# Attention tower on one core: another hand-written order of stages on five engines, the gate product as one multiplication and one sum, parts of row maxima taken by a maximum over one element

## What is computed

```python
h = emb_weight[x] + (lora_A[:, x] @ lora_B) * 2.0
n = layernorm(h)
q, k, v = split(n @ Wqkv + bqkv)                # 32 sequences x 512 tokens x 16 heads of 16
s_local  = where(abs(i - j) <= 64, q @ k.T / 4, -inf)
s_global = q @ k[:64].T / 4
gate = sigmoid(n @ Wg + bg)                     # the gate product: one number a token
o = (1 - gate) * softmax(s_local) @ v + gate * softmax(s_global) @ v[:64]
h = h + o @ Wout + bout
r = layernorm(h)                                # router: top 2 of 8, rank in the expert, slot
h = h + combine(experts(dispatch(r, top2)), p)
```

## Time and profile before

| | |
|---|---|
| median of 3 runs | 4156.22 us (4153.16 to 4160.92) |
| the profiled execution's own time | 4118.99 us |
| its span, first to last instruction | 4117.1 us |
| attention phase with the pipeline full | 337.8 to 2249.2 us, 26 periods |
| expert phase | from about 2529 us to the end |
| busy in the span | PE 89%, PEld 71%, POOL 56%, DVE 54%, ACT 48% |

### The profile page before, as it was taken

One profiled execution on the slowest core, in us unless ns is written; L12 is line 12 of the kernel. 1 busy time (PEld: TensorE's weight loads), 2 busy tenths in 40 slices (PEclk: granted clock), 3 DMA queues, 4 the chain that ended last, 5 costly groups with the idle time before them and its releaser, 6 DMA issues. The chain is left out here.

```text
span 4117.1 us, 119187 instructions
## 1 busy us (share of the span) xinstructions
PE 3647.8 (89%) x47729; PEld 2913.1 (71%) x47730; DVE 2204.4 (54%) x5585; ACT 1987.2 (48%) x3119; POOL 2296.8 (56%) x2659
## 2 busy tenths in 40 slices
PE   2798888888898888988889875999999998999998
PEld 1455555555555555555555555999999998999998
DVE  4476666666667575675666643343433343443333
ACT  0465555555555555555555543444444443444343
POOL 2466665766657666676676654444444444444443
PEclk8798888889889898898889977999999999999999
DMA  5443443444444344443444413232323232322222
GB/s 119 125 146 115 133 124 123 134 120 130 127 122 140 114 138 120 130 132 115 134 124 138 126 43 103 46 67 46 69 46 68 45 68 46 67 48 46 46 45 40
DMA packets 240810, 397.78 MB, mean 97 GB/s; under 512 B 34692, under 2 KB 148820, under 8 KB 240244
## 3 DMA queue, kind: packets, MB, share of 16 engines
q1 hardware_dynamic: 167908, 299.07, 23.9%
q0 software_dynamic: 70512, 91.16, 12.8%
q10 hardware_dynamic: 1952, 1.31, 0.2%
HBM read 198.55 MB, written 192.88 MB: 95 GB/s over the span
## 5 line engine op out<-in xcount | busy, mean ns | idle before, releaser
L1332 POOL DMA_INDIRECT out_y<-out_t,tok_out x264 | 424.9, 1610 | 772.8 <-DMA out_y<-out_t,tok_out 398.6
L1478 ACT ACTIVATE act<-psS 128x512 f32<-128x512 f32 x528 | 316.0, 599 | 907.0 <-PE psS L1406 902.8
L864 ACT ACTIVATE pl<-psS 128x896 f32<-128x896 f32 x512 | 467.6, 913 | 498.0 <-PE psS L712 432.9
L951 DVE TENSOR_REDUCE negm<-psS 128x4 f32<-128x640 f32 x512 | 417.8, 816 | 484.3 <-PE psS L686 271.9
L1540 DVE TENSOR_TENSOR h_lo<-act,h_hi 128x512 fp32r<-128x512 f32 x528 | 367.8, 697 | 574.7 <-ACT h_hi L1479 560.3
L541 POOL TENSOR_SCALAR_AFFINE_SELECT pl<-pl 128x512 f32<-128x512 f32 x512 | 334.7, 654 | 608.0 <-ACT pl L864 607.2
L1441 PE MATMUL psO<-w_hi,h_hi 128*128 128x256 f32 x2112 | 598.7, 283 | 1.1 <-DVE h_lo L1540 1.1
L1441 PE MATMUL psO<-w_lo,h_hi 128*128 128x256 f32 x2112 | 588.7, 279 | 0.0
L1441 PE MATMUL psO<-w_hi,h_lo 128*128 128x256 f32 x2112 | 587.6, 278 | 0.0
L1406 PE MATMUL psS<-xg_hi,w_hi 128*128 128x256 f32 x1984 | 551.7, 278 | 0.0
L1406 PE MATMUL psS<-xg_hi,w_lo 128*128 128x256 f32 x1984 | 551.5, 278 | 0.0
(11 more groups left out here) (230 smaller groups left out, 8118.8 us busy)
## 6 DMA issues: line engine op xcount, KB each, us to landing
qk_scr<-qk SPq DMA_DIRECT2D x64, 768.0 KB
Q<-qk_scr SPq DMA_DIRECT2D x128, 384.0 KB, 4.0
K<-qk_scr SPq DMA_DIRECT2D x128, 384.0 KB, 4.8
qk_scr<-qk SPq DMA_DIRECT2D x64, 512.0 KB
qk_scr<-qk SPq DMA_DIRECT2D x64, 256.0 KB
h_rows<-held SPq DMA_DIRECT2D x32, 512.0 KB
hb<-h_rows SPq DMA_DIRECT2D x32, 512.0 KB, 4.3
out_y<-h SPq DMA_DIRECT2D x32, 512.0 KB
```

The source lines that it names most:

```text
L864: act.activation(pl[:, v, half, :, lo:hi], psS[:, 0:2, lo:hi], ACT.Exp, scale=SCALE).then_inc(exp_done, 1)
L951: dve.tensor_reduce(negm[:, g, 0, v, :, 2 * half:2 * half + 2], psS[:, 2:4, 0:2 * BAND].rearrange("p a (q u) -> p a q u", u=BAND), AX.X, A ...
L1332: pool.indirect_dma_start(out=y[:, :], in_=out_t[:, tile.out, s, :], in_offset=None, out_offset=bass.IndirectOffsetOnAxis(ap=tok_out[:, ti ...
L1478: act.activation(act32[:, b, :, 0:cols], src, ACT.Silu)
```

## The change

It has three parts. All five tables `ORDER` are written anew; the stages of a period stay the same but for `zgate`, and the tables begin at another point of the period. The gate product, four instructions that multiply and sum 256 values each, becomes one multiplication of 1024 values (`zgate` 0) and one sum (`zgate` 1). Two of the four steps of `cut` turn from a copy with conversion into a maximum over an axis of one element, which gives the same numbers.

```diff
-                            act.wait_ge(zgate_done, QB * (s + 1))
+                            act.wait_ge(zgate_done, s + 1)
...
-                            dve.tensor_copy(m_cut[:, 0, :, :], whole).then_inc(k_cut, 1)
+                            dve.tensor_reduce(m_cut[:, 0, :, :], whole.unsqueeze(3), AX.X, ALU.max).then_inc(k_cut, 1)
...
-                            dve.tensor_copy(m_cut[:, 1, :, :], m_rest[:, :, :]).then_inc(k_cut, 1)
+                            dve.tensor_reduce(m_cut[:, 1, :, :], m_rest[:, :, :].unsqueeze(3), AX.X, ALU.max).then_inc(k_cut, 1)
...
                             if arg == 0:
                                 dve.wait_ge(xn_done, QB * (s + 1))
+                                dve.tensor_tensor(xn_wg[:, :, :], xn[:, :, :], wg_b[:, :].unsqueeze(1).to_broadcast([P, QB, D]),
+                                                  ALU.mult).then_inc(xn_wg_done, 1)
+                            else:
+                                dve.wait_ge(xn_wg_done, s + 1)
                                 need(dve, egate_done, s)
-                            dve.tensor_tensor_reduce(out=xn_wg[:, arg, :], in0=xn[:, arg, :], in1=wg_b[:, :], scale=1.0,
-                                                     scalar=0.0, op0=ALU.mult, op1=ALU.add,
-                                                     accum_out=zgate[:, arg:arg + 1]).then_inc(zgate_done, 1)
+                                dve.tensor_reduce(zgate[:, :], xn_wg[:, :, :], AX.X, ALU.add).then_inc(zgate_done, 1)
...
-                ("cur", "sel", 8), ("nxt", "hold", 1), ("nxt", "hold", 2), ("nxt", "hold", 3), ("cur", "sel", 10), ("cur", "sel", 11),
+                ("cur", "sel", 10), ("cur", "sel", 11), ("cur", "sel", 12), ("cur", "sel", 13), ("cur", "sel", 15), ("cur", "sel", 16),
```

More of the change, by code:

```diff
@@ L445, in build @@
             ORDER["pe"] = (
[L446 to L457, removed]
@@ L458, in build @@
-                ("cur", "exp", 17), ("nxt", "max", 8), ("prev", "router", None), ("cur", "exp", 18), ("nxt", "values", 0),
-                ("nxt", "max", 9), ("cur", "exp", 19), ("nxt", "values", 1), ("cur", "out", 9), ("nxt", "max", 10), ("cur", "out", 10),
+                ("cur", "max", 15), ("cur", "exp", 2), ("prev", "mix", 1), ("cur", "max", 16), ("cur", "exp", 3), ("cur", "out", 0),
+                ("cur", "exp", 4), ("cur", "max", 17), ("prev", "mix", 2), ("cur", "exp", 5), ("cur", "max", 18), ("cur", "exp", 6),
@@ new lines, in build @@
+                ("cur", "out", 1), ("cur", "exp", 7), ("cur", "max", 19), ("cur", "m_rows", 2), ("cur", "exp", 8), ("prev", "mix", 3),
+                ("cur", "out", 2), ("cur", "exp", 9), ("cur", "out", 3), ("past", "ahead", None), ("cur", "m_rows", 3),
+                ("prev", "attn_t", 0), ("prev", "attn_t", 1), ("far", "embed", None), ("prev", "project", 0), ("prev", "project", 1),
+                ("nxt", "max", 0), ("cur", "exp", 10), ("cur", "out", 4), ("cur", "exp", 11), ("nxt", "max", 1), ("far", "lora", 0),
@@ new lines, in build @@
+                ("nxt", "values", 0), ("nxt", "max", 9), ("prev", "router", None), ("nxt", "values", 1), ("nxt", "max", 10),
+                ("cur", "out", 10), ("cur", "out", 11), ("nxt", "values", 2), ("nxt", "m_rows", 1), ("nxt", "max", 11),
+                ("far", "xn_t", 0), ("far", "xn_t", 1), ("nxt", "max", 12), ("far", "qk", 0), ("far", "qk", 1), ("nxt", "max", 13),
+                ("far", "qk", 2), ("far", "qk", 3), ("nxt", "exp", 0), ("nxt", "max", 14), ("cur", "mix", 0), ("nxt", "exp", 1),
@@ new lines, in build @@
+                ("cur", "exp", 17), ("cur", "evac", (2, 0)), ("cur", "exp", 18), ("prev", "x2_t", 1), ("nxt", "m_rows", 0),
+                ("cur", "exp", 19), ("nxt", "values", 0), ("cur", "evac", (2, 1)), ("far", "std1", None), ("nxt", "values", 1),
+                ("nxt", "values", 2), ("nxt", "m_rows", 1), ("far", "xn_t", 0), ("far", "xn_t", 1), ("far", "qk", 0), ("far", "qk", 1),
+                ("cur", "evac", (3, 0)), ("far", "qk2", 0), ("far", "qk2", 1), ("cur", "evac", (3, 1)), ("far", "qk", 2),
@@ new lines, in build @@
+                ("far", "qk", 3), ("nxt", "exp", 0), ("nxt", "exp", 1), ("prev", "weights", None), ("far", "qk2", 2), ("far", "qk2", 3),
+                ("nxt", "exp", 2), ("nxt", "exp", 3), ("nxt", "exp", 4), ("nxt", "exp", 5), ("nxt", "exp", 6), ("nxt", "exp", 7),
+                ("nxt", "m_rows", 2), ("nxt", "exp", 8), ("nxt", "evac", (0, 0)), ("nxt", "evac", (0, 1)), ("nxt", "exp", 9),
+                ("nxt", "m_rows", 3), ("cur", "attn_t", 0), ("cur", "attn_t", 1), ("next", "embed", None), ("nxt", "exp", 10),
@@ L473, in build @@
+                ("far", "gate", None),
             )
             ORDER["dve"] = (
[L475 to L478 removed]
@@ L492, in build @@
[L492 to L493 removed]
+                ("nxt", "qk", 2), ("nxt", "qk", 3), ("cur", "max", 14), ("cur", "cut", (2, 0)), ("prev", "mix", (0, 0)),
+                ("prev", "mix", (0, 1)), ("prev", "mix", (0, 2)), ("cur", "max", 15), ("cur", "cut", (2, 1)), ("cur", "cut", (2, 2)),
@@ L512, in build @@
+                ("far", "load", 3), ("far", "m_in", 0), ("far", "m_out", 1), ("cur", "y", None),
             )
```

76 lines of the change are left out of this document (34 added, 42 removed).

## The result

The changed kernel took **4180.21 us** (median of 5 runs, 4176.72 to 4186.38), the one before 4156.22 us (4148.71 to 4160.92) beside it: a ratio of **1.0062 [1.0047, 1.0077]**, 24 us slower. Forecast were 4104 us. The later runs met a surprise that belongs here: chips are of two kinds for this kernel (so the text calls them; the runs don't show whether it is the chip itself). On **kind A** the kernel before takes 4104 to 4156 us (the chip above, and that of the g runs); on **kind B** it takes 3933 to 3944 us (three chips), and there the changed kernel is faster: 0.9927 [0.9900, 0.9953] and 0.9897 [0.9874, 0.9920]. The expectations call A slow and B quick. So the question became why this order loses on A what it wins on B.

What follows compares the result with a forecast made beforehand. No engine is full; the attention period of 73.5 us bounds: PE's work, waits and low clock. Terms -2.8 - 0.7 + 0.7 - 0.8 + 1.6 = -2.0 us, times 26 = -52 us, give 4104 us; range 4050 to 4182.

Steps and rivals of the forecast that it cites:

- The run's rule: POOL's indexed transfers in a row: three are free, each further 1 us costs about 1.08 us of ACT's hole.
- Six become four, gain 2.8, with 1.4 of hole left: POOL's six transfers become four gathers after `sel` 16: gain 2.8 us a period, bounds 0 and 4.2.
- Five scatters in a light stretch, loss 0.7: Five scatters between `sel` 8 and `sel` 10, beside lighter PE work: loss 0.7 us a period, bounds 0 and 2.8.
- Exponentials closer together, +1.6: PE waits for ACT at four more places between `exp` stages, 0.4 us each: loss 1.6 us a period, bounds 1.3 and 3.5.
- Rival C: Slower: closer exponentials cost 0.87 us each and turn periods into the long, low-clock kind; 4192 us, chance 0.14.
- The wait for `mix` before `m_rows` 2, gain 0.8: PE's wait of 1.53 us for DVE at L778 shrinks by 0.8 a period; bounds gain 1.5, loss 0.7.
- The edits on DVE, nothing: New gate product priced equal, bound 0.5 us a period; cuts off the path, priced nothing, bound a gain of 0.3.
- The clock: How much of a period runs at 1.2 GHz, left unplaced: 1.5 us a period, 40 us either way.
- Rival D: The hole isn't POOL's: PE runs dry from its own dense stretch; 21 us slower, 4177 us, chance 0.08.
- The stated signs: Right: periods 71 to 72 us, ACT's hole under 6. Wrong: hole of 7 or more, or PE waiting for `max`.
- B, "the five scatters starve PE like the six": No net change: the five scatters starve PE too, so 2.1 us a period come back; 4159 us, chance 0.14.
- Starved supply of instructions: PE gets instructions more slowly while POOL issues indexed transfers: 94 in 4 us during the six, against 258 needed when dense.

Runs made afterwards that it cites:

- g runs: Group of follow-up runs on one kind A chip, where the kernel before takes 4103.67 us; changed orders and operations were timed against it.
- h1: The changed kernel, unchanged, a third time, on kind B: 3901.19 us against 3944.26 for the kernel before, ratio 0.9897.
- h5: The kernel before with the new gate product alone (one multiplication, one sum), on kind B: 3952.81 us against 3944.26, ratio 1.0017.
- g4: The kernel before's order with the new operations and POOL's run of six transfers taken apart, on kind A: 3965.19 us, 0.9646 of the kernel before.
- g3: The changed kernel with POOL's list respread, no more than two transfers in a row, residual ahead of gathers, on kind A: 4022.99 us, 0.9785 of before.
- e1: The kernel before's order on all engines with the new gate product and cuts, on kind B: 3904.48 us, 0.992 of the kernel before.
- g1: The kernel before, unchanged, run for its profile on another kind A chip: 4116.06 us in one run, beside 4103.67.
- f3: The changed kernel with a POOL subtraction in place of each attention-phase transfer with indices, on kind B: 3898.67 us, 0.9923 of the kernel before.

## Why the prediction was wrong

**The run's rule, "about 1.08 us of hole for 1 us of run beyond three".** This step failed. Its two points were read rightly. That a run of three is free, and that five cost next to nothing where PE's work is light, was not right: on kind A what falls due in a run mostly waits for its end and about 1 to 1.4 us more, at both points and at all three runs of the new order (the table above). What that costs PE shows beside h1, which has the same program on kind B: the time between fixed places of PE's list, mean of the 26 periods in us, with the terms that came from the rule. The places are the first matmuls of `embed` (L809), `lora` 0 (L815), `x2_t` 0 (L835), `router` (L842) and `xn_t` 0 (L822).

| stretch of PE | run in it | forecast cost | after, A | h1, B | more on A |
|---|---|---|---|---|---|
| L809 to L815 | five scatters | 0.7 | 9.70 | 6.99 | 2.7 |
| L835 to L842 | four gathers | 1.4 | 16.42 | 11.98 | 4.4 |
| L842 to L822 | `gather` 5, 6, `scatter` 1 | none | 9.39 | 7.92 | 1.5 |
| the rest | none of three or more | | 40.18 | 38.83 | 1.3 |

- *Six become four, gain 2.8, with 1.4 of hole left.* The hole itself is as the rule has it, 4.1 + 1.4 = 5.5 us, and 5.2 to 5.5 were measured in 18 periods. Its price is not: 4.4. Half of that is idle time of PE (4.16 us against 1.88), half is busy time (12.26 against 10.10) at a mean clock of 0.83 instead of 0.93.
- *Five scatters in a light stretch, loss 0.7.* Measured 2.7; `out` 4 alone takes 3.42 us instead of 0.99. I had counted what PE needs in supply. The stretch may be light for PE, but the first thing due behind it is due all the same.
- *`gather` 5, `gather` 6 and `scatter` 1.* I gave them no term at all, since a run of three was free by the rule. PE's wait for `values` there is up to 2.57 us and has 42.8 / 26 = 1.6 us a period.

The old order pays for its one run too: beside h5 (B, its tables) the stretch L815 to L835 with the six takes 16.77 us against 11.35, and the next one, L835 to L842, 6.56 against 4.33, at a clock of 0.62 instead of 1.00. By whole periods kind A costs the old order 73.5 - 67.9 = 5.6 us and the new one 75.7 - 65.7 = 10.0. That is 4.3 us more, and the forecast missed by 4.2: on B the period fell by 2.1 us from h5 to h1, next to the forecast -2.0. That nearness is luck, since the terms were read from rows of kind A. That the whole of the 5.6 and 10.0 us comes from the runs isn't shown; that taking them apart gives back 4.5 us a period (117 us) in the old order and about as much in the new one is (g4, g3).

**Exponentials closer together, +1.6.** On kind B nearly exact: L712 and L719 wait (76.6 + 16.0 + 12.7) / 26 = 4.05 us a period for ACT in h1, and in the old order 2.45 in h5 (24.0 + 39.6 us in 26 periods) or 2.67 in e1 (28.5 + 41.0). On A it is 5.97 against 1.54, +4.4. Of that 1.5 is L719, with waits up to 4.1 us, which were 1.5 at most. All 18 of its waits of 2 us or more stand right behind the four gathers, where ACT is late itself, so this part belongs to the run (it lies in the 4.4 above). Rival C's sign, an L712 wait over 100 us, did not come true in the full periods, for which 17.5 us had been read: 76.8 us, or 93.3 with the waits for L868 (100.1 for L864 in the whole run). Nor did its second half: the clock went up and not down.

**The wait for `mix` before `m_rows` 2, gain 0.8.** The mechanism was right, and the whole 1.53 went.

**The edits on DVE, nothing.** The gate product: right (h5). The multiplication of 1024 elements, which no row had, takes 1.21 us, as taken. The cuts: mis-sized, 22 us on A (0.85 a period) where the bound was 0.3, since the saving was priced by its own length and not by what it moves behind it. The long mean of L1055 in the earlier trace rows was the sign. In the new order it overlaps with the gain before, since both are the same wait.

**The clock.** Left open, bounded at 40 us. It rose from 0.87 to 0.93 and gave back 48.8 us of PE's busy time; without it the kernel after would have lost more. The mean hides that in the stretch with the gathers it is 0.83.

**POOL as the cause.** Rival D, that the hole isn't POOL's, has the nearest time (4177) with the wrong reason: the same PE work without the run beside it (g4, on A) has no such hole. The stated signs worked: PE hardly waits for a `max` (5.6 us in 3 waits), but the mean period (71 to 72 forecast) and the longest holes (ACT 6.7 us, beside the scatters; DVE 7.3 us, in 3 periods) pointed to B, "the five scatters starve PE like the six", which had 0.14.

**Open.** What the kinds are (chip, memory, something of the moment), and by what way a run of transfers holds up engines that have nothing to do with it. Starved supply of instructions, as the prediction had it, fits the stretched L740 and the issue time; a late signal fits `values`, where PE's record shows no gap between 1625.5 and 1630.2, and `exp` 15 before, whose last matmuls end at 1643.80 while ACT starts at 1645.19. No run here tells them apart.

## What to carry over

Read a hole's end as well as its length, and in all periods: if it ends at a fixed distance behind another engine's run, as here in 26 of 26, suspect that even a short run costs, and try taking the runs apart before moving them to a lighter place. An edit's own saving is a poor bound for it where a tiny instruction behind it can meet another engine's run, as the 0.17 us that became 1.50. And a change of 1% in a kernel whose stalls hang on the chip should be timed on several chips.

## What was unexpected of the hardware

- The same kernel takes 4104 to 4156 us on some chips and 3933 to 3944 us on others, with equal durations of POOL's transfers (0.97 us) and of ACT's and DVE's instructions (0.92 and 0.82 us). Most of the difference lies in the attention phase, beside the transfers and in the granted clock there (0.88 in g1, 0.94 in h5, with nearly the same tables): of the 146 us between their 26 full periods 106 are busy time of PE.
- A multiplication of 32 elements with both inputs in SBUF takes 0.17 to 2.68 us, as POOL's selections let it. The Trainium skill says in "SBUF — State Buffer", section "Who interferes with whom", that a VectorE instruction with two inputs in SBUF contends with a GpSimd instruction that reads SBUF. The trace agrees: 2.68 us in h5, to the end of the fourth selection, and 1.50 us before, to the end of the second. I had read there for the cast only.
- The same section says that a transfer never contends with a compute engine. On kind B f3 bears that out in effect, 3898.67 against 3895.38 us. On kind A the place of the transfers is worth 117 us (the gate product in it taken as nothing), though the runs don't show that it is the transfer and not its issue on POOL.
